# Inverse square root of the query and key variances: one GpSimd power in place of ScalarE's logarithm and exponential and GpSimd's Newton step

## The reference

```python
def _layernorm(t, g, b):                      # over the 16 channels of a head
    m = jnp.mean(t, axis=-1, keepdims=True)
    v = jnp.mean(jnp.square(t - m), axis=-1, keepdims=True)
    return (t - m) * jax.lax.rsqrt(v + EPS) * g + b
...
q = _layernorm(q, gq, bq)
k = _layernorm(k, gk, bk)
scores = jnp.einsum('nhld,nhmd->nhlm', q, k) * SM_SCALE      # causal softmax, times v
return out @ Wo.T + bo
```

## Time and profile before

| | |
|---|---|
| median of 3 runs | 4086.57 us (4073.86 to 4089.9) |
| the profiled execution | 4099.86 us, span 4098.0 us |
| granted TensorE clock, mean | 0.924 of full speed |
| TensorE (PE) busy | 3508.8 us, 86% |
| VectorE (DVE) busy | 3057.7 us, 75% |
| ScalarE (ACT) busy | 2302.6 us, 56% |
| GpSimd (POOL) busy | 805.5 us, 20% |

### The profile page before, as it was taken

How to read it: one execution, slowest core, us unless ns; L and a number is a source line. 1 busy time by engine, 2 the same in 40 slices (tenths; PEclk the granted TensorE clock), 3 DMA queues, 4 the chain that set the end, 5 groups by cost and what they waited for, 6 DMA issues and landing times.

```text
span 4098.0 us, 93072 instructions
## 1 busy us (share of the span) xinstructions
PE 3508.8 (86%) x31392; PEld 2764.5 (67%) x31392; DVE 3057.7 (75%) x6444; ACT 2302.6 (56%) x6346; POOL 805.5 (20%) x951
## 2 busy tenths in 40 slices
PE   3898888989889898897988989888898888989888
PEld 2676766767667676676766767667676766767667
DVE  3778777687777877778777687877878777787776
ACT  2655546565465654646646466554656546565464
POOL 1212222022220222202222122221212222022220
PEclk9899999999999998999989989999999999999999
DMA  3000000000000000000000000000000000000000
GB/s 73 7 2 7 7 7 7 2 7 7 7 7 2 7 7 7 7 1 12 2 7 7 7 7 2 7 7 7 7 2 7 7 7 7 2 7 7 6 2 6
DMA packets 33906, 30.35 MB, mean 7 GB/s; under 512 B 8864, under 2 KB 33312, under 8 KB 33376
## 3 DMA queue, kind: packets, MB, share of 16 engines
q1 hardware_dynamic: 33376, 23.68, 2.0%
HBM read 15.28 MB, written 8.39 MB: 6 GB/s over the span
## 4 chain that ended last, share of the span: by engine, by line
PE 57%; issue 14%; DVE 12%; ACT 10%; POOL 5%; SPq 1%; ACTq 0%; DVEq 0%; DMA 0%; POOLq 0%
PE bank L625 12%; PE scores L723 9%; ACT prob L839 6%; PE bank L636 6%; PE scores L612 6%; PE bank L735 4%; PE scores L613 4%; PE scores L614 3%; PE bank L596 2%; POOL qf L503 2%; PE scores L697 2%; PE scores L608 2%; PE scores L677 2%; DVE negmax L1055 1%; PE bank L555 1%
## 5 line engine op out<-in xcount | busy, mean ns | idle before, releaser
L839 ACT ACTIVATE prob<-scores,negmax 128x128 f32<-128x128 f32 (+3 forms) x2048 | 1060.7, 538 | 221.8 <-DVE negmax L1055 178.6
L1055 DVE TENSOR_REDUCE negmax<-scores 128x1 f32<-128x128 f32 (+3 forms) x2048 | 885.4, 484 | 101.0 <-PE scores L614 87.6
L625 PE MATMUL bank<-ident,prob 128*128 128x128 f32 x5120 | 730.8, 280 | 44.9 <-DVE probt L1063 35.6
L1063 DVE COPY probt<-bank 128x512 f32<-128x512 f32 x896 | 597.5, 685 | 179.2 <-PE bank L625 172.2
L625 PEld LDWEIGHTS bank<-ident,prob 128*128 128x128 f32 x5120 | 548.2, 142 | 156.0 <-DVE probt L1063 66.3
L614 PE MATMUL scores<-mask,ident 128*128 128x128 bf16 x2048 | 450.0, 231 | 0.0
L612 PE MATMUL scores<-khh,qt 128*128 128x256 f32 (+2 forms) x1024 | 438.4, 429 | 13.3 <-ACT qt L810 7.5
L839 ACT ACTIVATION_READ_ACCUMULATOR prob<-scores,negmax 128x1 f32 x2048 | 437.6, 214 | 0.0
L810 ACT ACTIVATE probt<-bank 128x512 f32<-128x512 f32 x384 | 233.0, 607 | 205.6 <-PE bank L625 205.6
L613 PE MATMUL scores<-kll,qt 128*128 128x256 f32 (+2 forms) x1024 | 345.4, 337 | 0.0
L596 PE MATMUL bank<-ident,stk 128*128 128x128 bf16 x2048 | 203.8, 286 | 153.2 <-DVE stk L1153 122.2
(11 more groups left out here) (179 smaller groups left out, 6967.4 us busy)
## 6 DMA issues: line engine op xcount, KB each, us to landing
x_in<-in_x_rows SPq DMA_DIRECT2D x16, 512.0 KB, 3.5
out_rows<-x SPq DMA_DIRECT2D x16, 512.0 KB, 3.6
r_gu<-in_wg SPq DMA_DIRECT2D x2, 512.0 KB, 5.0
r_gu<-in_wu SPq DMA_DIRECT2D x2, 512.0 KB, 5.5
r_d<-in_wd SPq DMA_DIRECT2D x1, 1024.0 KB, 6.8
r_wqt<-in_wq_nope_t SPq DMA_DIRECT2D x1, 512.0 KB, 6.2
r_wqr<-in_wq SPq DMA_DIRECT2D x2, 256.0 KB, 8.8
r_wob<-in_wo SPq DMA_DIRECT2D x1, 512.0 KB, 5.3
```

The lines of the kernel that those rows point to most:

```text
L625: ins = nc.tensor.transpose(bank[4 + n % 2][:, q * P:(q + 1) * P], prob[:, u % 2, q, i * P:(i + 1) * P], ident[:, :])
L839: nc.scalar.activation(prob[:, u % 2, q, 0:n], bank[q][:, 0:n], ACT.Exp, bias=negmax[:, a, u, q:q + 1], accum_out=sums[:, a, u, q:q + 1]). ...
L1055: nc.vector.tensor_reduce(negmax[:, a, u, M * part:M * part + M], scores[:, M * part:M * part + M, 0:n], axis=AX.X, op=ALU.max, negate=Tru ...
L1063: nc.vector.tensor_copy(probt[:, u % 2, i], bank[4 + n % 2][:, :]).then_inc(probt_dve.sem, 1)
```

## The change

GpSimd computes `rq = ssq ** -0.5` in a single `tensor_tensor` with the power as its operation, over 128x32, the exponent column of `expo` broadcast over the 32 columns. ScalarE's logarithm and exponential and GpSimd's four instructions go, with the signal `root_ready` and the buffer `lnv`; `rq` has one slot a buffer instead of four. GpSimd now waits for `ssq_ready` directly. VectorE waits, before it overwrites `ssq` of a buffer, until the power that reads it is done.

```diff
-    lnv = new("lnv", [P, 2, 2 * H], F32)
-    rq = new("rq", [P, 2, 4, 2 * H], F32)
+    rq = new("rq", [P, 2, 2 * H], F32)
...
             for t in range(NT):
                 s = t % 2
 
-                pool.wait_ge(root_ready.sem, root_ready.at(b, t + 1))
-                y, y2, w = rq[:, s, 0], rq[:, s, 1], rq[:, s, 2]
-                chain.link(nc.gpsimd.tensor_tensor(y2, y, y, ALU.mult))
-                chain.link(nc.gpsimd.tensor_tensor(w, y2, ssq[:, s], ALU.mult))
-                settle(pool, pool_passed)
-                chain.link(nc.gpsimd.tensor_scalar(y2, w, -0.5, 1.5, ALU.mult, ALU.add))
+                pool.wait_ge(ssq_ready.sem, ssq_ready.at(b, t + 1))
                 if t >= 2:
                     pool.wait_ge(qn_ready.sem, qn_ready.at(b, t - 1))
-                nc.gpsimd.tensor_tensor(rq[:, s, 3], y, y2, ALU.mult).then_inc(rq_ready.sem, 1)
+                nc.gpsimd.tensor_tensor(rq[:, s], ssq[:, s], expo[:, 0:1].to_broadcast([P, 2 * H]), ALU.pow).then_inc(rq_ready.sem, 1)
...
             for step in range(NT + 3):
-                t = step - 1
-                if 0 <= t < NT:
-                    s = t % 2
-
-                    act.wait_ge(ssq_ready.sem, ssq_ready.at(b, t + 1))
-                    chain.link(nc.scalar.activation(lnv[:, s], ssq[:, s], ACT.Ln))
-                    if t >= 2:
-                        act.wait_ge(rq_ready.sem, rq_ready.at(b, t - 1))
-                    nc.scalar.activation(rq[:, s, 0], lnv[:, s], ACT.Exp, scale=-0.5).then_inc(root_ready.sem, 1)
...
                     dve.wait_ge(sq_ready.sem, sq_ready.at(b, t + 1))
+                    if t >= 2:
+                        dve.wait_ge(rq_ready.sem, rq_ready.at(b, t - 1))
                     chain.link(nc.vector.reduce_sum(ssq[:, s], sq[:, s].rearrange("p (h d) -> p h d", d=D), axis=AX.X))
...
-                       rq[:, s, 3].unsqueeze(2).to_broadcast([P, 2 * H, D]), ALU.mult).then_inc(qn_ready.sem, 1)
+                       rq[:, s].unsqueeze(2).to_broadcast([P, 2 * H, D]), ALU.mult).then_inc(qn_ready.sem, 1)
```

More of the change, by code:

```diff
@@ L263, in _build @@
     ssq_ready = Signal(sem("ssq_ready"), NT)
-    root_ready = Signal(sem("root_ready"), NT)
     rq_ready = Signal(sem("rq_ready"), NT)
@@ L324, in _build @@
     pool_link = sem("pool_link")
-    act_link = sem("act_link")
-    DVE_LINKS, POOL_LINKS, ACT_LINKS = 28, 18, 4
+    DVE_LINKS, POOL_LINKS = 28, 6
     block = ctx.enter_context(nc.Block())
@@ L806, in _ @@
     def _(act):
-        chain = Chain(act, act_link, ACT_LINKS)
         def copy(out, in_, **k):
@@ L879, in sequence @@
         def sequence(b, last):
-            chain.start(b)
             for step in range(NT + 3):
-                t = step - 1
-                if 0 <= t < NT:
-                    s = t % 2
-                    act.wait_ge(ssq_ready.sem, ssq_ready.at(b, t + 1))
-                    chain.link(nc.scalar.activation(lnv[:, s], ssq[:, s], ACT.Ln))
-                    if t >= 2:
-                        act.wait_ge(rq_ready.sem, rq_ready.at(b, t - 1))
-                    nc.scalar.activation(rq[:, s, 0], lnv[:, s], ACT.Exp, scale=-0.5).then_inc(root_ready.sem, 1)
                 t = step
@@ L967, in sequence @@
             act.preload_act_table_set("natural_log_exp_and_others")
-            chain.end(last)
         split_tokens(0, 0)
```

## The result

The changed kernel is slower: 4294.2 us (4292.85 to 4297.63, 4 runs) against 4082.44 us of the kernel before in the same comparison (4 runs). The ratio is 1.0521, 95% interval 1.0497 to 1.0545, so +212 us. It lies inside the stated range, 146 us under the stated value.

What follows compares the result with a forecast made beforehand. The stage before attention, wholly on the path, was taken to be led by GpSimd's loop with four powers: 22 us a sequence, 352 us in all, on 4086.57 us gives 4439, stated as 4440 us; range 4115 to 4550 us.

Steps and rivals of the forecast that it cites:

- The bound and the chain: Query/key projection to first score, 16 times: lies wholly on the path; grows 22 us a sequence, 352 us in all.
- What hides the removed work: ScalarE's logarithms and exponentials, 29 us in all, and waits moved two tiles back: both costed at nothing.
- The power's length: GpSimd's new power over 128x32, one per tile: 6.8 us each, four powers 27.2 us a sequence.
- The exclusion: VectorE instructions with two SBUF inputs wait for GpSimd's whole power; waits for `qn` together 5.6 us a sequence.
- The alternative that I priced at 56 us less: The power holds VectorE back only at its start: 3.5 us a sequence less, 296 us in all, 4383 us.
- Starts behind VectorE: GpSimd powers that meet a VectorE instruction in progress wait too: three, 0.3 us each, 0.9 us a sequence.
- The sum: GpSimd's powers, gain and offset pairs and waits added up: through at 388.5 us instead of 366.5, 22.0 us later.
- linear case: All of the power's arithmetic on GpSimd is paid per column: 4383 to 4529 us; chance 0.60.
- partly fixed case: Rival: half of the power's 0.82 us is setup, 3.9 us a power, 166 us slower, 4253 us; chance 0.23.
- What follows GpSimd: Tile 3's copies, residue, stack and transposes, 7.8 us to the first score: shrinks about 0.7 us, grows as much.
- Fixed: Rival: GpSimd's power takes about 1.1 to 1.5 us, no change, 4087 to 4106 us; chance 0.14.
- Faster: Rival: GpSimd's power at 0.27 us saves 2.7 us a sequence, 43 us, giving 4043 us; chance 0.03.

## Why the prediction was right, point by point

- **The bound and the chain.** Right: the stage grew from the loop on GpSimd, by its full length, and no later work hid it. The 16 stages give 206 us in the profiles. That the rest stayed as it was is right for its work and not quite for its time: it was 13 us shorter in the profiled pair, with a higher clock in the projections of the second attention. That 206 us come close to the 212 us of the medians is in part chance.
- **What hides the removed work.** Right on ScalarE (put back, it costs nothing) and on the moved waits: GpSimd waited ahead of a power only for the first variances of a sequence, 16 times, never for `qn`.
- **The power's length, taken as 6.8 us.** The mis-sized term. It is 5.5 us, with 0.38 us fixed and 0.157 us a column. The linear reading was right. The error was the fixed part: 0.20 us, the plain product's, where the power has 0.38 us, so each of four columns was charged 0.205 us instead of 0.157, and a factor of eight carried that to 1.3 us a power. Four powers: 27.2 us predicted, 22.0 found.
- **The exclusion.** Wrong, the second step that failed. I let the power hold VectorE's gain for its whole length as the product holds L1149. L1123 takes 0.69 us (L1141 of before; I had written 6 to 7), begun 0.8 us into the second power. The three waits for `qn` are 0.8 us each, 2.4 us instead of 5.6. The Trainium skill (SBUF — State Buffer, "Who interferes with whom") has the pair of ports held for the whole instruction; beside a product the traces agree (1.56 us for the residue), beside a power they do not (0.67 us). The alternative that I priced at 56 us less, without this exclusion, is the true one.
- **Starts behind VectorE.** 0.3 us for three powers, 0.9 us; found 0.19 us for two (5.60 instead of 5.41), which the 22.0 us contain.
- **The sum.** 42.8 us from the first variance to the last offset were predicted, 33.5 found: 5.2 us from the power's length, 3.2 from the exclusion, 0.9 from the starts. All three erred to the same side, so none made good another; the forecast of 352 us was 1.7 times the 212 us measured, and 4294 us lies under all that the linear case alone allowed (4383 us and more). The range held it because it was kept open down into the partly fixed case; that is width, not foresight. What follows GpSimd was taken as unchanged, a gain of 0.7 us against as large a loss to the clock. The gain did not come (from the last offset to the last piece of the stack 4.46 us, before 4.47); the loss was 0.45 us. Together 22 us predicted and 13.2 found a sequence. (The upper end of the linear case adds up to 4528 us, not 4529.)
- **The rivals.** *Partly fixed* (0.61 us fixed and 0.10 us a column) was right that the fixed part is larger than a product's, and too low with 3.9 us a power. *Fixed* and *faster* did not happen, but shorter instructions in the power's place tell what they would have given. For a power of 1.1 to 1.7 us "no change" holds (4 and 8 columns: ratios 0.9992 and 0.9988). *Faster*, at the product's length, was priced at 43 us and is refuted at 0.9996: VectorE's queue stands in the way of GpSimd's saving, as its 0.33 us of idle time had suggested, and half of what is left goes to a longer tail.
- **The profile after.** Foreseen and found: the new line, x64 (5.5, not 6 to 8 us), and VectorE's new wait for it. GpSimd's busy time was to rise by 360 us and rose by 270; the stage was to be 52 us and is 44. L1141 at 6 to 7 us was not found (0.69 us). The clock was not lower in the stage's second half (0.69 as before) but in its first (0.74, before 0.84) and in the slice of the last transposes.

## What to carry to other kernels

When one instruction replaces several, ask for its length at this width, and get two widths of the same operation before scaling: a fixed part that is off by 0.2 us became 1.3 us over a factor of eight. Then find how long it may be before it leads: here a power of up to 1.7 us was free (up to about 2.4 us by estimate) and each microsecond beyond cost four a sequence, while anything shorter gained nothing, since VectorE was the bound. Taking work off GpSimd alone gained nothing; moving it to VectorE, cutting GpSimd's instructions up, or handing a piece to ScalarE at the price of two hops made the kernel slower. A saving of half a microsecond ahead of a burst of matmuls can be given back by the clock at which the burst runs. And before a sum over stages is called the whole difference, set it beside the spans of the two profiles that it was read from: here 206 us stood against 193, not 212.

## What the runs showed of the hardware that was not expected

- A power on GpSimd takes 0.38 us plus 0.157 us for each column of 128 partitions, 75 times the slope of a plain product (0.0021 us from the earlier trace rows), whatever the base (0.1, 2.0 or the variances).
- While it runs, VectorE's instructions with two SBUF inputs and its casts go at full speed (0.67 and 0.43 us), though a product on GpSimd holds the same ones back by 0.9 us and more. A power over 32 columns that starts as VectorE is in such an instruction is itself delayed by 0.2 to 0.3 us; short ones at such a place took up to 0.8 us longer.
